# Set-up products of the second and third cross-attention moved from the expert loop, the second block and the dense units to one piece behind the first router

## The reference, cut to what matters

```
x = x + attn0(layernorm(x), ctx)    # 16 heads of 8, no biases
x = x + moe0(layernorm(x))          # 8 experts, top 2, GELU, f = 512
x = x + attn1(layernorm(x), ctx)    # one head of 128, biases bq, bk, bv
x = x + moe1(layernorm(x))          # 8 experts, top 2, relu, f = 256, biases
x = x + attn2(layernorm(x), ctx)    # 16 heads of 64, masked by i == j mod n
x = x + conv_ffn(layernorm(x))      # quantised, depthwise convolution over 3 taps
x = x + attn3(layernorm(x), ctx)    # 16 heads of 8, biases bq, bk, bv, bo
x = x + moe3(layernorm(x))          # 8 experts, top 2, gated (silu), f = 512
```

## Time and profile before

| what | us |
|---|---|
| runs (3): median, lowest, highest | 679.75, 679.54, 680.88 |
| profiled execution: its time, its span | 682.17, 680.3 |
| busy: PE, DVE, ACT, POOL | 576.5, 437.6, 233.0, 207.7 |
| mean granted TensorE clock | 0.895 |

### The profile page before, as it was taken

How to read it: one execution, slowest core, us unless ns; L and a number is a source line. 1 busy time by engine, 2 the same in 40 slices (tenths; PEclk the granted TensorE clock), 3 DMA queues, 4 the chain that set the end, 5 groups by cost and what they waited for, 6 DMA issues and landing times.

```text
span 680.3 us, 12175 instructions
## 1 busy us (share of the span) xinstructions
PE 576.5 (85%) x3853; PEld 478.4 (70%) x3854; DVE 437.6 (64%) x1576; ACT 233.0 (34%) x515; POOL 207.7 (31%) x258
## 2 busy tenths in 40 slices
PE   5799817879997999999998679989996369999993
PEld 2477703769995568888987557746776159899993
DVE  8878883214365665566687686787778837555573
ACT  2355201235553423444433033325541013333331
POOL 6100057744557024920000000000000778733332
PEclk9899657979996999989989888989995579989997
DMA  9999922212254000000000350021000122211243
GB/s 220 184 185 248 267 75 63 67 52 72 71 151 141 0 2 1 1 1 1 1 0 1 119 129 1 1 82 44 1 1 0 52 59 62 62 47 47 56 123 112
DMA packets 61016, 47.67 MB, mean 70 GB/s; under 512 B 6266, under 2 KB 54819, under 8 KB 60806
## 3 DMA queue, kind: packets, MB, share of 16 engines
q1 hardware_dynamic: 56422, 37.68, 24.2%
q0 software_dynamic: 4544, 9.38, 4.1%
HBM read 27.53 MB, written 19.51 MB: 69 GB/s over the span
## 4 chain that ended last, share of the span: by engine, by line
PE 53%; issue 20%; SPq 12%; DVE 10%; another core or an unknown queue 2%; ACT 1%; DMA 1%; DVEq 0%; POOL 0%; POOLq 0%; ACTq 0%
PE bank L2186 16%; PE bank L2197 9%; PE bank L1826 7%; SPq L420 7%; PE bank L2008 5%; SPq L409 2%; SPq L414 2%; PE bank L1815 2%; PE bank L1816 2%; PE bank L1817 2%; PE bank L2174 2%; DVE X L1397 1%; DVE XW L991 1%; PE bank L1851 1%
## 5 line engine op out<-in xcount | busy, mean ns | idle before, releaser
L590 POOL DMA_INDIRECT xw<-XW,slot_i x64 | 62.4, 975 | 317.6 <-DVE slot_i L1149 296.7
L2186 PE MATMUL bank<-xT,wcur 128*128 128x128 f32 x936 | 124.5, 285 | 11.3 <-ACT xT L762 11.3
L2186 PEld LDWEIGHTS bank<-xT,wcur 128*128 128x128 f32 x936 | 117.3, 201 | 12.7 <-ACT xT L762 10.7
L606 POOL DMA_INDIRECT yt<-Y,dest_i x78 | 75.9, 973 | 90.0 <-ACT Y L775 44.6
L1257 DVE COPY wcur<-WA 128x512 f32 x78 | 37.8, 485 | 54.3 <-PE bank L2186 51.4
L1397 DVE SCALAR_TENSOR_TENSOR X<-bank,G,X 128x128 f32<-128x128 f32 x128 | 36.0, 344 | 47.4 <-PE bank L1826 38.7
L842 ACT ACTIVATE hT<-bank,b_cols 128x512 f32<-128x512 f32 x64 | 43.5, 687 | 65.7 <-PE bank L1817 65.2
L1826 PE MATMUL bank<-WC,hT 128*128 128x128 f32 x512 | 65.4, 283 | 0.0
L1826 PEld LDWEIGHTS bank<-WC,hT 128*128 128x128 f32 x512 | 62.6, 198 | 2.8 <-ACT hT L842 0.9
L1272 DVE TENSOR_TENSOR hT<-gb,bank 128x512 f32<-128x512 f32 x39 | 26.8, 688 | 44.5 <-ACT gb L767 38.6
L767 ACT ACTIVATE gb<-bank 128x512 f32<-128x512 f32 x39 | 23.3, 597 | 57.3 <-PE bank L2186 46.7
(11 more groups left out here) (390 smaller groups left out, 1142.4 us busy)
## 6 DMA issues: line engine op xcount, KB each, us to landing
xw<-pad_rows SPq DMA_DIRECT2D x34, 260.0 KB, 9.2
xrow<-xw SPq DMA_DIRECT2D x78, 65.0 KB
WA<-in_fc_dram SPq DMA_DIRECT2D x16, 256.0 KB, 6.5
YT<-yt SPq DMA_DIRECT2D x16, 256.0 KB, 2.9
WA<-in_pj_dram SPq DMA_DIRECT2D x8, 256.0 KB, 5.5
WB<-in_fc_dram SPq DMA_DIRECT2D x8, 256.0 KB, 4.6
WB<-in_pj_dram SPq DMA_DIRECT2D x8, 256.0 KB, 6.1
yt<-Y,dest_i POOLq DMA_INDIRECT x78
```

Source lines behind the costliest of these rows:

```text
L590: pool.indirect_dma_start(out=xw_dram, out_offset=bass.IndirectOffsetOnAxis(ap=slot_i[:, choice, tile:tile + 1], axis=0), in_=XW[:, tile, ...
L606: pool.indirect_dma_start(out=yt_dram, out_offset=bass.IndirectOffsetOnAxis(ap=dest_i[:, t:t + 1], axis=0), in_=Y[:, s, :], in_offset=None ...
L2186: ins = pe.matmul(dst, wcur[:, s4, at:at + P], xT[s4 % 2][:, :], start=True, stop=True)
```

## The change

A function `later_setup()` is added to PE, ACT and DVE, called behind the router and ahead of `experts(0)`. It holds all of `setup1`, the four products of `setup(1)`, the key rows and the values of attention 3, one behind another, in banks 4 to 7. At its end PE waits for ACT's copies of M and for DVE's values, since the banks are used next by the expert loop. The key rows `bq . k` are made with one product of 16 x 128 (`bq_heads`) in place of four of 4 x 512; their split into three bfloat16 parts goes from POOL to DVE, and they leave by a DMA that SP issues at slot 8 of the expert loop. The waits for `rows_out` in ACT, DVE and the wait for `r_read` in `weight_sums` go. PE's hardware loop now begins with round 1 and ACT's with its second round. POOL's `pause` clears a part of `mfill` in place of `M`.

```diff
@@ SP, in experts(layer), slot t
+                    if layer == 0 and t == ROWS_AT:
+                        sp.wait_ge(r_evac, 1)
+                        sp.dma_start(rows_dram.rearrange("i b (h k) -> h i b k", h=H),
+                                     rparts.rearrange("h i (b k) -> h i b k", b=B)).then_inc(rows_out, 16)
@@ SP, behind the loop
-            sp.wait_ge(r_evac, 1)
-            sp.dma_start(rows_dram.rearrange("i b f -> b i f"), rparts).then_inc(rows_out, 16)
@@ POOL
             pool.wait_ge(s1_evac, 6)
+            pool.wait_ge(rows_out, 16)
             pool.memset(GT8[:, :], 0.0).then_inc(cb_clear, 1)
-            pool.wait_ge(r_read, 1)
-            link(pool.tensor_copy(rparts[:, 0, :], rrow))
...
-            pool.tensor_copy(rparts[:, 2, :], rrow).then_inc(r_evac, 1)
@@ ACT
+            def later_setup():
+                keys = bank[4][:, 0:P].rearrange("p (b k) -> p b k", b=B)
+                act.wait_ge(in_small, 64)
+                act.wait_ge(s1_mm, 1)
+                act.activation(kT[:, :, :], keys, ACT.Identity, bias=bk1).then_inc(s1_evac, 1)
+                act.wait_ge(s1_mm, 2)
+                act.activation(V1[:, :, :], bank[5][0:K, :]...).then_inc(s1_evac, 1)
+                act.wait_ge(s1_mm, 5)
+                act.activation(M1...), (br_all...), (r1...), (b1_cols...)   # s1_evac each
+                act.wait_ge(setup_mm, B + 3)
+                act.activation(kT[:, :, :], keys, ACT.Identity, bias=bk3).then_inc(s1_evac, 1)
+                act.wait_ge(r_mm, 1)
+                act.activation(rrow, bank[4][0:H, P:2 * P], ACT.Copy).then_inc(r_read, 1)
+                setup(1, 5)
@@ ACT, second_block
-                setup(1)
...
-                    if u == 1:
-                        act.wait_ge(r_mm, 1)
-                        act.activation(rrow, bank[7][0:B, :], ACT.Copy).then_inc(r_read, 1)
...
-                        act.wait_ge(rows_out, 16)
@@ DVE
+            def later_setup():
+                dve.wait_ge(in_small, 64)
+                dve.tensor_scalar(bq_heads[:, :], head_mask[:, :], bq3, None, ALU.mult).then_inc(setup_evac, 1)
+                dve.wait_ge(s1_evac, 7)
+                for b in range(B):
+                    keys(1, b)
+                values(1)
+                dve.wait_ge(r_read, 1)
+                split3([rparts[:, i, :] for i in range(PARTS)], rrow).then_inc(r_evac, 1)
@@ PE
+            def later_setup():
+                pe.wait_ge(in_small, 64)
+                pe.matmul(bank[4][:, 0:P], wk1, ctxT, ...).then_inc(s1_mm, 1)
+                for b in range(B):
+                    ...   # values of attention 1: two products each, bank[5]
+                pe.wait_ge(s1_evac, 2)
+                ...   # M1, r1, br1, the turned bias, keys of attention 3 (wk3)
+                pe.wait_ge(s1_evac, 7)
+                pe.wait_ge(setup_evac, B + 2)
+                pe.matmul(bank[4][0:H, P:2 * P], bq_heads[:, :], keys, start=True, stop=True).then_inc(r_mm, 1)
+                setup(1, wq3, 5)
+                values(1, wv3)
+                pe.wait_ge(m_evac, 2 * B)
+                pe.wait_ge(setup_evac, 2 * B + 3)
@@ PE, second_block
-                setup(1, wq3)
...
-                    if u == 1:
-                        key_rows()
-                    if u == 2:
-                        pe.wait_ge(s2_act, 9)
-                        values(1, wv3)
                     if u == 3:
-                        pe.wait_ge(r_read, 1)
                         weight_sums()
                     if u == 5:
-                        pe.wait_ge(setup_evac, 2 * (B + 1))
+                        pe.wait_ge(s2_act, 9)
                         tokens1(2, bank[6])
@@ PE, experts
                 round_of(0, RING, first=layer == 0)
-                for i in range(1, 1 + pieces):
-                    setup1(i - 1)
+                with pe.Fori(1, ROUNDS) as i:
                     round_of(i, RING)
@@ PE, main
             router(0, 1, gate0)
+            later_setup()
             pe.wait_ge(in_experts[0], 16 * 2 * E)
             experts(0, [UP0], DOWN0)
```

117 lines of the change are left out of this document (36 added, 81 removed).

## The result

| | us |
|---|---|
| before (20 runs): median, lowest, highest | 680.76, 679.54, 683.04 |
| after (20 runs): median, lowest, highest | 684.64, 679.88, 689.41 |
| ratio after to before, 95% interval | 1.0053, 1.0036 to 1.0070 |
| profiled execution after: its time, its span | 684.45, 682.4 |

What follows compares the result with a forecast made beforehand. PE was taken to bound the expert loop, with one large hole. Start +5.6 and loop -4.2 (together +1.4), second block -2.2, dense units -4.2 gave -5.0: 679.75 to 674.8 us; own range 672.5 to 677.5, 8 in 10 667.3 to 679.4.

Steps and rivals of the forecast that it cites:

- the start of the loop: From the router to the first `dn_mm`: the added set-up delays it from 121.8 to 127.4, costing 5.6 us.
- the end of the set-up at 117.6: Behind the router: the `later_setup` chain takes 15.6 us from 101.0, plus 1.0 for cold PE.
- the 5.6 for the unread products: Between set-up and first turned tile: the 26 unread products take 5.6 us at full clock.
- my 123.2: Forecast time of the first turned tile, behind set-up and unread products, in place of 113.58.
- the rival in which the set-up meets the moves: Start: PE's results come through at a third of the rate; start costs 16.6, total 685.8 us; chance 0.11.
- From the first tile to the first `dn_mm`: Start of the expert loop: ACT's chain of copies, table load, GELU and one `up_mm` takes 4.2 us.
- The hole: Expert loop: ACT's 9.7 us without copies beside POOL's dense indirect DMAs, taken to stay as it is.
- The rival in which it closes with the pieces of set-up: Expert loop: the hole goes with the moved pieces, 8.5 us more gained, 666.3 us; chance 0.15.
- The loop's pieces: Expert loop: three set-up pieces of 3.1, 0.9 and 0.2 leave PE's row, gaining 4.2 us.
- The second block: `setup(1)` leaves PE's row between `projected(1)` and `summed`; the first token transpose comes 2.2 us earlier.
- The dense units: Key rows and values of attention 3 leave PE's row; the transposes at unit 5 come 4.2 us earlier.
- The rival of gains handed back: Second block or unit 5 waits for something else; half of 6.4 us stays, 678.0 us; chance 0.12.

Runs made afterwards that it cites:

- after_ref: The changed kernel, unchanged, run again for its trace in a group at the lower level; ratio 1.0013 to the kernel before at 663.7 us.
- after_again: The changed kernel, unchanged, run once more in another group at the lower level; 664.94 us, ratio 1.0018 to the kernel before at 664.7.
- before_ref: The kernel before, unchanged, run again for its trace in a group at the lower level; ratio 0.9989.
- stand_in: The changed kernel with unread products of the same length put where the moved work stood in PE's row; 672.99 us, ratio 1.0147 to the kernel before.
- only1: The kernel before with only attention 1's factors and attention 3's keys made behind the router, layer 0's unread products removed, weights first; ratio 0.9982.
- b_spaced3_c: The kernel before with a small memset before and behind each of layer 0's last eight scatters, third run, higher level; ratio 0.9966.
- spaced: The changed kernel with a small memset and its wait behind each of layer 0's first sixteen indirect DMAs, lower level; ratio 1.0037.

## Why the prediction was wrong

**The step that failed is the start of the loop**: +5.6 us forecast, +16.0 measured, and +12.3 or +10.9 where no report is late (`after_ref`, `after_again`). Within it the end of the set-up at 117.6 and the 5.6 for the unread products were wrong; the rest held. The first turned tile stands 10.8 us behind my 123.2:

- *The late copy: 5.8.* The unread products start at 126.66, in `after_ref` at 120.89, since ACT's copy starts at 111.96 there and at 106.11 here. I had this as the rival in which the set-up meets the moves, with 0.11, and its price, 16.6 for the start and 685.8 us in all, is close to what came (16.0 and 684.6). I argued it down because DVE follows PE's small products at once in the router, beside the same dense DMAs. That was evidence on DMAs up to 101 only; all late reports of the traces at that place begin behind 105. The trace also held one that I did not see, the first turned tile copied 2.2 us late: I read it as the wait for tile 1. It is shown that such waits come at the higher level alone. That dense DMAs cause them is supported for the loop's hole by one run; for the copy at the start it is argued by likeness, as the three runs that would test it fell at the lower level.
- *Cold PE in the set-up: 3.3* (120.89 against 117.6 at the lower level). I priced the passes by rows at full clock and added 1.0, for which I had no row. The sixteen passes of the values took 4.6 (101.20 to 105.77) in place of 2.66 and M 5.66 in place of 3.87, 3.7 together; the granted clock was 0.50 from 101 to 110. My own row said that this stretch was not warm.
- *The unread products: 1.7* (126.66 to 133.96 is 7.3, against 5.6). I expected full clock since PE would just have been busy for 14 us; for the first half of their time it was at 1.2 GHz. In `after_again` they took 5.77, as priced, and M took longer: this term and the last share the time that PE spends at 1.2 GHz.

These make the 10.8. From the first tile to the first `dn_mm` it took 3.9, with 4.2 forecast: that term held, but only because the unread products covered DVE's weights. I had called them useless behind the set-up. Removing them gave 4 us, not 5.6 to 7, so nearly half of their time was doing something.

**The hole** I took as it is, and it stayed (some 9 us in both). The rival in which it closes with the pieces of set-up failed: it needs neither them nor the place in the code. Where PE's next code would have been fetched, the transfers of the instruction queue say the same. Of `before`, the DMA queues between 126 and 140.2 (packets, MB, share of 16 engines),

```profile
q0 software_dynamic: 330, 0.70, 15.0%
q1 hardware_dynamic: 432, 0.20, 6.8%
```

and of `before_ref`, which has no hole there, the same stretch:

```profile
q0 software_dynamic: 352, 0.73, 15.8%
q1 hardware_dynamic: 864, 0.40, 13.1%
q8 instruction: 1, 0.02, 0.5%
```

No instruction fetch lies in the stretch with the hole, and one in the stretch without; the next one of `before` lies at 141.8, when ACT and PE have gone on. In `after` there is none between 106 and 112 either. By the rule of the Trainium skill that I weighed ("Runtime: NRT & Kernel Launch", instruction fetch mechanics), a taken branch out of the window waits for a fetch; this case's holes are not that.

**The loop's pieces** (4.2) gave 2.9 in the one pair, which has another remote wait of 2.3 near the loop's end, and 4.2 in the other. **The second block** (2.2) gave 3.9 and 4.0. In the lower pair 1.7 of that is the clock, as `before_ref` ran `projected(1)` in 3.68 and `after_ref` in 1.98, so 2.3 is left for the chain, as forecast. In the higher pair the 3.9 is another sum: up to `projected(1)` `after` gains 5.1, as PE no longer waits for DVE's tokens (0.97 and 2.19 in `before`) and is warmer, and from there on it loses 1.2, since `projected(1)` and `summed` are cold (3.78 and 3.65, against 1.98 and 1.88). **The dense units** (4.2) gave 3.5 and 2.9. The rival of gains handed back did not come true up to unit 5; `stand_in` shows some of it later on. Put 10.9 or 12.3 in the place of 5.6, and my sum of -5.0 becomes +0.3 or +1.7, with 16.0 it becomes +5.4; the medians have +0.3 to +0.9 at the lower level and +3.9 at the higher.

## What to carry to other kernels

Room between two stages is worth only its own length: measure it to the event that really ends it (here 12.5 us, to the landed tile), price what goes in at the clock and with the hand-overs of that stretch, and move what fits. Here all of the set-up with the filler behind it lost 3.9 us or nothing. Without the filler and with the weights first it gained 0.5 to 0.6%, and half of it, with the same two edits, 0.7 to 1.4%; which of the three edits does how much was not separated. Before a chain is put ahead of a stage, list what the other engines have queued behind it, and what the filler that is there was covering. A cause that the profile names "remote" must be priced wherever its conditions hold, not only where it was seen.

## What the runs showed of the hardware that I had not expected

- The same kernel takes 664 or 682 us for a whole group of runs, on one chip too. In `before` and `before_ref` (spans 680.3 and 663.4) 9 us of the 17 are in one hole behind PE's products while POOL issues indirect DMAs with 0.3 us between them, 3 to 4 beside the moves of the second loop, and 2 at the first tile. What sets the level is open.
- At the higher level the release does not come when the dense stretch ends: the sixteenth DMA ended at 108.78 in `after` and the copy started at 111.96; in `only1` at 109.38 and 115.49. With a memset of 0.55 us between the DMAs of the loop the hole stayed away in `b_spaced3_c`, but the first tile's copy was 2.8 us late there beside DMAs that were spaced too.
- Not only PE's reports are late at that level: in `only1` DVE waits 0.84 and 0.54 for its own last step at 106.15 and 106.87.
- The same 26 products behind a pause of 1.3 to 1.7 us took 7.4 to 7.5 us in five traces and 5.77 in two (`after_again`, `spaced`), and in those two the eight passes of M ahead of them took 6.25 and 6.40 in place of 5.5 to 5.8.
- Two versions beat both kernels: all set-up moved, without the unread products and with the weights first (0.9948 and 0.9936, at the lower level), and only attention 3's (0.9933 and 0.9865 at the higher, 0.9929 at the lower with the spacing). Which of them is better at one level wasn't measured.
